# The Mamba scan of a macaron block: two of sixteen products move to GpSimd, their decay to PSUM

## The reference

```
x = x + 0.5 * ffn(layernorm(x))        # FP4-quantised gate/up/down, silu
x = x + mixer(layernorm(x))            # the selective scan below
x = x + 0.5 * ffn(layernorm(x))
```

```
h[d,n] = exp(-delta[t,d]*a[d,n]) * h[d,n] + delta[t,d]*u[t,d]*B[t,n]
y[t,d] = sum_n h[d,n]*C[t,n] + D[d]*u[t,d]
out    = (y * silu(z)) @ out_proj
```

## Time and profile before

| what | us |
|---|---|
| median of 3 runs | 3248.5 (3247.22 to 3249.37) |
| the profiled execution | 3248.44 |
| its span in the profile | 3246.6 |
| first product to last scan of the mixer | 746.9 to 2626.9 |
| VectorE busy in the span | 2650.3 |
| GpSimd busy in the span | 2175.2 |
| TensorE busy in the span | 2717.0 |
| ScalarE busy in the span | 1705.8 |

### The profile page before, as it was taken

One profiled execution on the slowest core, in us unless ns is written; L12 is line 12 of the kernel. 1 busy time (PEld: TensorE's weight loads), 2 busy tenths in 40 slices (PEclk: granted clock), 3 DMA queues, 4 the chain that ended last, 5 costly groups with the idle time before them and its releaser, 6 DMA issues. The chain is left out here.

```text
span 3246.6 us, 31734 instructions
## 1 busy us (share of the span) xinstructions
PE 2717.0 (84%) x10349; PEld 1394.6 (43%) x10349; DVE 2650.3 (82%) x2498; ACT 1705.8 (53%) x2427; POOL 2175.2 (67%) x1219
## 2 busy tenths in 40 slices
PE   2999999776878878978978978878867659999998
PEld 1565556452324424424414424424422125655555
DVE  6777777407999999999999999999999946777775
ACT  3444444335665756666666666666654513444443
POOL 4566666306787877877777787777787735555652
PEclk9999999987888978979978978978966669999999
DMA  3011111108678687686776776767767720110100
GB/s 103 20 49 40 49 49 39 43 13 195 155 174 198 158 194 179 163 199 167 175 189 172 179 191 165 187 167 176 189 164 187 188 75 14 33 33 26 32 26 20
DMA packets 173304, 387.82 MB, mean 119 GB/s; under 512 B 22502, under 2 KB 90150, under 8 KB 172902
## 3 DMA queue, kind: packets, MB, share of 16 engines
q1 hardware_dynamic: 155382, 367.06, 45.5%
q10 hardware_dynamic: 17776, 18.94, 2.0%
HBM read 308.26 MB, written 52.49 MB: 111 GB/s over the span
## 5 line engine op out<-in xcount | busy, mean ns | idle before, releaser
L971 POOL TENSOR_TENSOR mix_scan<-mix_scan,mix_bc 128x1024 f32<-128x1024 f32 x512 | 1204.6, 2355 | 396.0 <-DVE mix_scan L1126 395.3
L1126 DVE TENSOR_TENSOR_SCAN mix_scan<-mix_decay,mix_ps_du 128x1024 f32<-128x1024 f32 x512 | 1170.0, 2285 | 63.1 <-ACT mix_decay L1072 20.6
L1138 DVE TENSOR_TENSOR mix_ps_du<-mix_ps_du,mix_bc 128x1024 f32<-128x1024 f32 x512 | 618.2, 1207 | 134.6 <-PE mix_ps_du L1239 134.0
L1239 PE MATMUL mix_ps_du<-mix_stack,mix_sel 96*128 96x512 bf16 x1024 | 366.6, 446 | 376.5 <-DVE mix_scan L1126 355.0
L716 PE MATMUL ffn_ps_gate_up<-ffn_w_gate_up,ffn_xT 128*128 128x512 f32 (+1 forms) x1536 | 656.5, 564 | 14.3 <-DVE ffn_h L480 14.0
L1072 ACT ACTIVATE mix_decay<-mix_decay,mix_a_neg 128x1024 f32<-128x1024 f32 x512 | 573.7, 1141 | 114.2 <-DMA mix_decay<-delta_rows 113.2
L755 PE MATMUL ffn_ps_down<-ffn_w_down,ffn_hT 128*128 128x256 f32 (+1 forms) x1536 | 382.4, 391 | 12.1 <-ACT ffn_hT L639 12.1
L716 PEld LDWEIGHTS ffn_ps_gate_up<-ffn_w_gate_up,ffn_xT 128*128 128x128 f32 x1536 | 273.1, 191 | 259.6 <-issue 218.3
L1239 PEld LDWEIGHTS mix_ps_du<-mix_stack,mix_sel 96*128 96x128 bf16 x1024 | 78.6, 103 | 685.6 <-DVE mix_scan L1126 554.9
L612 POOL TENSOR_TENSOR ffn_h_scaled<-ffn_h,ffn_h_recip 128x1408 f32<-128x1408 f32 x64 | 188.3, 2943 | 235.4 <-ACT ffn_h_recip L689 235.4
L1221 PE MATMUL mix_ps_y<-mix_scan,mix_red 128*32 128x512 f32 x2048 | 340.3, 747 | 4.8 <-POOL mix_scan L971 4.8
(11 more groups left out here) (136 smaller groups left out, 3712.8 us busy)
## 6 DMA issues: line engine op xcount, KB each, us to landing
mix_decay<-delta_rows SPq DMA_DIRECT2D x512, 512.0 KB, 7.1
mix_stack<-mix_parts SPq DMA_DIRECT2D x384, 64.0 KB, 2.0
delta_rows<-mix_delta SPq DMA_DIRECT2D x32, 512.0 KB, 3.1
ffn_x<-_attn_hidden_states_dram SPq DMA_DIRECT2D x32, 256.0 KB, 3.1
after_ffn<-ffn_y SPq DMA_DIRECT2D x32, 256.0 KB, 3.2
normed_ffn<-ffn_y_normed SPq DMA_DIRECT2D x32, 256.0 KB, 3.2
mix_x_tokens<-normed_ffn SPq DMA_DIRECT2D x32, 256.0 KB, 12.1
mix_x_residual<-after_ffn ACTq DMA_DIRECT2D x32, 256.0 KB, 4.0
```

Of the source, the lines that this page charges most:

```text
L971: G.tensor_tensor(wt, wt, bc[:, r % 2, 1, :], ALU.mult).then_inc(hc_done, 1)
L1126: V.tensor_tensor_scan(w[:, slot % RING, :], da[:, slot % SPREADS, :], ps_du[:, slot % 2, :], 0.0, ALU.mult, ALU.add).then_inc(scan_done, 1)
L1138: V.tensor_tensor(ps_du[:, slot % 2, :], ps_du[:, slot % 2, :], bc[:, r % 2, 0, :], ALU.mult)\
L1239: ins = M(ps_du[:, slot % 2, h * 512:(h + 1) * 512], const.sel[0:SEL, i, :], stack[:, c % 2, q, h * 512:(h + 1) * 512], start=True, stop=True)
```

## The change

In slots s = 3 and s = 15 of every chunk (64 of the 512 slots) the product with B is GpSimd's. TensorE does not replicate for these slots and VectorE makes no product for them. Instead SyncE keeps the last 32 rows of `delta*u` in DRAM (`keep_du`, once a chunk, at s = 5), and spreads 8 of them straight into the ring tile of the slot (`spread_du`, issued three slots ahead, behind that slot's `spread_delta`, once `y_made` says that the tile is free). GpSimd multiplies that tile by B in place, two slots ahead, in front of its C product of the slot. The decay of such a slot is written by ScalarE to the free half of `ps_du`, one slot ahead instead of two, after scan n-2. The scan then reads the decay from PSUM and the product from the ring tile that it writes.

```
+POOL_SLOTS = (3, 15)
+POOL_ROWS = 96
...
+            def keep_du(b, c):
+                sy.wait_ge(du_done, chunk(b, c))
+                sy.dma_start(du_dram[c % 2, :, :], du[POOL_ROWS:P, :]).then_inc(du_kept, 16)
+
+            def spread_du(r, R, slot):
+                c, s = divmod(slot, SLOTS)
+                sy.wait_ge(du_kept, 16 * chunk(R, c))
+                if slot >= RING or r > 0:
+                    sy.wait_ge(y_made, R * 16 + (slot - RING) // 4 + 1)
+                row = 32 * (s % 4) + 8 * (s // 4) - POOL_ROWS
+                sy.dma_start(w[:, slot % RING, :],
+                             du_dram[c % 2, row:row + NCH, :].unsqueeze(0).to_broadcast([NST, NCH, L]))\
+                  .then_inc(du_spread[(by_pool(R, slot) - 1) % 2], 16)
...
                         if s - LATER[c] == SCALE:
                             keep_delta(b, rb % 2, cc)
+                        if s - LATER[c] == SCALE + 1:
+                            keep_du(b, cc)
...
                     if core(rr, full):
                         spread_delta(rr, R2, at)
+                    if core(r, full) and s + 3 in POOL_SLOTS:
+                        spread_du(r, R, slot + 3)
...
+                    if core(r, full) and s + 2 in POOL_SLOTS:
+                        n = by_pool(R, slot + 2)
+                        pool.wait_ge(du_spread[(n - 1) % 2], 16 * ((n + 1) // 2))
+                        if slot + 2 < SLOTS:
+                            pool.wait_ge(taken["B"], (R + 1) * 4)
+                        wt = w[:, (slot + 2) % RING, :]
+                        G.tensor_tensor(wt, wt, bc[:, r % 2, 0, :], ALU.mult).then_inc(pool_dbu, 1)
                     if core(r, full):
                         pool.wait_ge(scan_done, R * 64 + (slot + 1))
...
                         if s - LATER[c] == REST1:
                             pool.wait_ge(cast1, n)
+                            pool.wait_ge(du_kept, 16 * n)
...
+            def decay(r, R, at, c, s):
+                act.wait_ge(spread_in[at % SPREADS], 16 * (R * (64 // SPREADS) + (at // SPREADS + 1)))
+                qi = 16 * c + 4 * (s % 4) + s // 4
+                to = da[:, at % SPREADS, :]
+                if s in POOL_SLOTS:
+                    act.wait_ge(scan_done, R * 64 + (at - 1))
+                    to = ps_du[:, at % 2, :]
+                A.activation(to, da[:, at % SPREADS, :], ACT.Exp, scale=const.aneg[:, qi:qi + 1]).then_inc(exp_done, 1)
...
+                    for by in (LEAD - 1, LEAD):
+                        rr, R2, at = ahead(r, R, slot, by)
                         c2, s2 = divmod(at, SLOTS)
+                        if core(rr, full) and by == (LEAD - 1 if s2 in POOL_SLOTS else LEAD):
+                            decay(rr, R2, at, c2, s2)
...
+                if slot % SLOTS in POOL_SLOTS:
+                    dve.wait_ge(pool_dbu, by_pool(R, slot))
+                    state = w[:, slot % RING, :]
+                    V.tensor_tensor_scan(state, ps_du[:, slot % 2, :], state, 0.0, ALU.mult, ALU.add)\
+                     .then_inc(scan_done, 1)
...
+                    if core(r, full) and s not in POOL_SLOTS:
+                        dve.wait_ge(rep_du, R * 64 + (slot + 1) - by_pool(R, slot))
...
             def replicate(r, R, slot):
 
                 c, s = divmod(slot, SLOTS)
+                if s in POOL_SLOTS:
+                    return
```

More of the change, by code:

```diff
@@ L848, in mixer @@
         delta_dram = nc.dram_tensor("delta_rows", [2, DI, L], F32, kind="Internal").ap()
+        du_dram = nc.dram_tensor("delta_u_rows", [2, P - POOL_ROWS, L], F32, kind="Internal").ap()
         S = a.sem
@@ L866, in mixer @@
         y_made, yg_done = S("y_made"), S("gate_done")
+        du_kept, du_spread, pool_dbu = S("delta_u_kept"), [S(f"delta_u_spread{k}") for k in range(2)], S("pool_dbu")
         res_in, out_stored = [S(f"res_in{k}") for k in range(4)], [S(f"out_stored{k}") for k in range(4)]
@@ L907, in chunk, with by_pool @@
             return b * CHUNKS + (c + 1)
+        def by_pool(R, slot):
+            c, s = divmod(slot, SLOTS)
+            return (R * CHUNKS + c) * len(POOL_SLOTS) + sum(t <= s for t in POOL_SLOTS)
         @block.sync
@@ L1066, in program @@
                             take(r, full, R, kind, rel, n, bank)
-                    rr, R2, at = ahead(r, R, slot, LEAD)
-                    if core(rr, full):
-                        act.wait_ge(spread_in[at % SPREADS], 16 * (R2 * (64 // SPREADS) + (at // SPREADS + 1)))
+                    for by in (LEAD - 1, LEAD):
+                        rr, R2, at = ahead(r, R, slot, by)
                         c2, s2 = divmod(at, SLOTS)
-                        qi = 16 * c2 + 4 * (s2 % 4) + s2 // 4
-                        A.activation(da[:, at % SPREADS, :], da[:, at % SPREADS, :], ACT.Exp,
-                                     scale=const.aneg[:, qi:qi + 1]).then_inc(exp_done, 1)
+                        if core(rr, full) and by == (LEAD - 1 if s2 in POOL_SLOTS else LEAD):
+                            decay(rr, R2, at, c2, s2)
                     if (full or r >= 1) and slot in STORE_SLOTS:
@@ L1122, in scan @@
                 dve.wait_ge(exp_done, n)
[L1123 to L1126, removed]
-                                     ALU.mult, ALU.add).then_inc(scan_done, 1)
+                if slot % SLOTS in POOL_SLOTS:
[3 more added lines that the diff above has]
+                     .then_inc(scan_done, 1)
+                else:
+                    dve.wait_ge(dbu_done, n - by_pool(R, slot))
+                    if slot >= 8 or r > 0:
+                        dve.wait_ge(y_made, R * 16 + (slot - 8) // 4 + 1)
+                    V.tensor_tensor_scan(w[:, slot % RING, :], da[:, slot % SPREADS, :], ps_du[:, slot % 2, :], 0.0,
+                                         ALU.mult, ALU.add).then_inc(scan_done, 1)
             def program(r, R, full):
@@ L1132, in program @@
                     c, s = divmod(slot, SLOTS)
-                    if core(r, full):
-                        n = R * 64 + (slot + 1)
-                        dve.wait_ge(rep_du, n)
+                    if core(r, full) and s not in POOL_SLOTS:
+                        dve.wait_ge(rep_du, R * 64 + (slot + 1) - by_pool(R, slot))
                         if slot == 0:
```

## The result

The changed kernel takes 3441.1 us (3438.5 to 3451.3, 4 runs) against 3248.0 of the kernel before on the same chip: 1.060 times as long, 95% interval 1.0578 to 1.0622. The direction was forecast; the time lies 59 us above the 3382 predicted and 1 us above the upper end of the range.

The account below looks back on a forecast made before the run. VectorE's stream of products and scans was taken to bound the mixer, at 3.5 us a slot. +189 - 38.6 - 26 + 8 + 4 = +136 us on 3248.4 gave 3384, rounded down to 3382; range 3320 to 3440.

Parts of the forecast that it names:

- Products removed: On VectorE, the path bounding the mixer: 64 products of 1.207 us go away, 77.2 us, the whole gain on offer.
- Products added to GpSimd, at 0: On GpSimd: 64 products of 2.355 us add 151 us of work, still fit, and cost 0.
- Rival 2: GpSimd's late C products delay the third part, lengthening the burst and next stall: 3413 to 3475 us, chance 0.08.
- The new transfer for s=15: At 31 chunk seams: it lands behind the decay burst, VectorE stalls 6.1 us on average, +189 us.
- Rivals 1 and 3: Rival 1: transfer comes in time, 3218 us or 3171, chance 0.07; rival 3: no measurable change, chance 0.02.
- The estimate of 3.2 us: For the 512 KB transfer of s=15: about 2 us plus bytes over 436 GB/s, which would mean no stall.
- What the stall covers: VectorE's existing waits for TensorE and decays at the seam, such as slot 16, disappear behind the stall: -26 us.
- The new transfer for s=3, at 0: Queued behind slot 22's decay transfer, it arrives in time for scan 19: 0, or up to 1 us.
- The decay for s=3: ScalarE makes it one slot later, behind TensorE's jobs: +1.0 us a batch, +8 in all, ends -39 and +40.
- 4 for the lag: GpSimd's lag reaching s=9 makes the third part and burst late: 4 us on the total, 0 to 30.
- `keep_du` at 0: On SyncE: one decay transfer comes 3.6 us later, for a scan nine slots on, costing 0 us.
- the scan and exponential with changed places at 0: Swapping PSUM and SBUF operands leaves their times unchanged; bounds +-6 us over 64 scans.

Follow-up runs that it names:

- e7: Changed kernel with both delta*u transfers (s=15, s=3) issued ahead of the decay transfers and the decay made before the slot's jobs: 3173.0 us, 0.976 of the kernel before.
- e1: Changed kernel with the s=15 transfer of delta*u issued before the burst of decay transfers: 3324.8 us, 1.0231 of the kernel before.
- e2: The change for s=15 alone, s=3 left as in the kernel before: 3411.1 us, 1.0493 of the kernel before.
- e6: The change for s=15 alone, plus six extra TensorE matmuls at the end of each slot s=15: 3380.6 us, 1.0393 of the kernel before.
- e4: Changed kernel with ScalarE making the decay before the slot's jobs, in slots before s=3 or s=15: 3409.3 us, 1.0489 of the kernel before.
- e10: Changed kernel plus six extra TensorE matmuls at the end of each slot s=15: 3399.5 us, 1.046 of the kernel before.
- e11: Changed kernel with both the six extra TensorE matmuls and the decay made ahead of the slot's jobs: 3377.6 us, 1.0393 of the kernel before.
- e8: Changed kernel with both delta*u transfers issued ahead of the decay transfers, the decay still behind the jobs: 3249.0 us, 0.9998 of the kernel before.
- e9: Changed kernel with both transfers early and the two slots' decay left in SBUF, made two slots ahead: 3235.3 us, 0.9943 of the kernel before.

## Why the prediction was wrong

The direction was right, and so was the stall that makes up most of the loss. By the predicted steps:

- *Products removed* (77.2 us): right as work, VectorE's busy time fell by 73. That e7 gets just 77 us is luck, as its slots show.
- *Products added to GpSimd, at 0*: right. Rival 2 (the lag feeds itself) falls: the transfers of the third part start 6.85 us after the scan of s=9 in both kernels (mean over three chunks of batches 1 to 6).
- *The new transfer for s=15*: right in place, cause and size: 18.3 us a batch for 18.8, and the transfers of s=15 land in 10.9 us for about 12. Rivals 1 and 3 fell. The estimate of 3.2 us from the Trainium skill's page SBUF — State Buffer is not met in e7 either: the shortest landing of its new transfers is 4.28 us.
- *What the stall covers*: right in size, 3.3 us a batch, but not in cause (and half of 28.9 + 20.6 is 24.8, not 26). In e7 there is no stall at slot 15, and the wait at slot 16 is gone all the same. TensorE is earlier before any stall begins: the projection that it makes ahead of slot 16's replication takes 3.78 us in the kernel before, at a granted clock of 0.50, and 1.99 in the kernel after, at 1.00. The rows that the prediction rests on thus held a price of the clock that it didn't see.

```profile
1505.08 3.78 PE L1171 MATMUL mix_ps_job<-mix_hnT,mix_w_in 128*128 128x256 f32 x8
```

```profile
1585.76 1.99 PE L1218 MATMUL mix_ps_job<-mix_hnT,mix_w_in 128*128 128x256 f32 x8
```

- *The new transfer for s=3, at 0*: right only because the stall at s=15 stood before it. e1 took that cover away, and s=3 rose by 8.8 us a batch. The prediction had not priced it without the cover.
- *What the stall does to the slots behind it*: here it failed first. The sum has a term for waits that the stall covers and none for waits that it makes; all of TensorE's times come from rows without such a stall. e2 has the stall as forecast and nothing changed at s=3 to 5, and still these slots take 5.6 us a batch more; it lies 38 us over the terms for s=15. Behind the stall TensorE ran for long stretches at its lower level, and its jobs, sums and replications took up to twice as long. e6 takes 30.5 us of e2's time away by keeping TensorE busy.
- *The decay for s=3*: the other failure, of size. The step "In chunk 1 ... the scan starts 2.0 later than today. In chunks 2 and 3 ... half of that" comes to +8 us, with 4 for the lag; on top of e2 s=3 costs 30. ScalarE takes TensorE's jobs ahead of this decay, so their lateness goes into it: scan 51 waited 8.07 us where the step allowed about 2. With both steps s=3, 4 and 5 took 8.2 us a batch more, for +1.0 in the sum. e4 puts the decay's place at 32 us, e10 TensorE's clock at up to 42, e11 both at 64.
- *`keep_du` at 0, the scan and exponential with changed places at 0*: right (2.289 for 2.285; 1.115 for 1.141).

The two failures make up 56 of the 59 us (38 + 18); 2.4 are the rounding down of the sum. One bound of the prediction was also off: with 40 in place of 8 for s=3 the upper one is 3414, not 3422.

e8 against e7 puts the decay's place at 76 us, e4 against the changed kernel at 32. A part of the difference is known: at s=15 the stall hides the decay, and without it e8 waits 2.9 us a batch more than e7, as the prediction's "about 3 us a batch" has it. What stays open is the rest, how the 64 us divide in the changed kernel, and how much of e10's 42 us is loss made good and how much a clock better than the kernel before had.

## What to carry to other kernels

Work that goes to an idle engine brings a transfer with it, and that transfer's time is its place in a queue: look for the burst ahead of it, not for the average share. A stall costs more than itself: what TensorE does around it can run at a lower clock, so a sum that adds a stall to rows of a kernel without stalls can be too low, by 38 us in e2. Read the granted clock beside each wait in the rows, too: a wait that goes away may have been the clock's. A change that loses 6% can be the right one in the wrong order: here three instructions moved in two engines' orders turned 3441 us into 3173.

## What the runs showed of the hardware that was not expected

- Six matmuls more at each of 32 seams made the kernel 42 us faster (e10): TensorE's granted clock from scan 47 to 51 went from 0.56 to 1.00.
- A scan with both inputs in SBUF takes 2.265 to 4.482 us beside GpSimd's products, by how much of a product is left at its start; one with one input in PSUM takes 2.26 to 2.29 (e9, e7).
- Decay transfers that land in 9.7 us in place of 7.1 cost nothing where they are issued six slots ahead: the scans' waits for them are 4.8 us in all (e7).
